# Shift rows of the first attention by one direct transfer, with one step less of lead

## The reference, cut to what matters

```python
qkv = x @ w_qkv.T                       # 16 heads, each with two sub-heads of width 4
def sdpa(qi, ki):
    s = jnp.einsum('bnhd,bmhd->bhnm', qi, ki) * scale
    p = jax.nn.softmax(s, axis=-1)
    return jnp.einsum('bhnm,bmhe->bhne', p, v)
o = sdpa(q[:, :, :, 0], k[:, :, :, 0]) - lam * sdpa(q[:, :, :, 1], k[:, :, :, 1])
```

## Time and profile before

| | |
|---|---|
| three runs | 1088.93, 1092.47, 1094.38 us (median 1092.47) |
| the profiled execution | 1090.65 us, its span 1088.8 us |
| busy over the span | PE 92%, DVE 88%, ACT 82%, POOL 45% |
| maxima on DVE | 512, 1208 ns each |
| exponentials on ACT | 1024, 600 ns each |
| first and last score matmul | 62.2 us, 652.6 us |

### The profile page before, as it was taken

How to read it: one execution, slowest core, us unless ns; L and a number is a source line. 1 busy time by engine, 2 the same in 40 slices (tenths; PEclk the granted TensorE clock), 3 DMA queues, 4 the chain that set the end, 5 groups by cost and what they waited for, 6 DMA issues and landing times.

```text
span 1088.8 us, 21671 instructions
## 1 busy us (share of the span) xinstructions
PE 1001.9 (92%) x8016; PEld 515.6 (47%) x8016; DVE 959.6 (88%) x1186; ACT 890.0 (82%) x1466; POOL 485.9 (45%) x893
## 2 busy tenths in 40 slices
PE   6389999999999999999999999999899999999998
PEld 3022222222222222222222236787677777777876
DVE  7799999999999999999999947798866988787665
ACT  5179999999999999999999987777775787678765
POOL 3363555455555544564556467342413431323331
PEclk9579999999999999999999999999999999999999
DMA  8911110111011101100110008575757466757763
GB/s 277 304 30 50 52 51 4 50 51 51 4 51 51 37 17 51 51 26 28 52 51 22 3 8 192 144 187 131 173 150 179 136 160 179 194 145 182 197 190 90
DMA packets 80473, 108.91 MB, mean 100 GB/s; under 512 B 23536, under 2 KB 33520, under 8 KB 80368
## 3 DMA queue, kind: packets, MB, share of 16 engines
q1 hardware_dynamic: 66336, 100.98, 34.4%
q10 hardware_dynamic: 14032, 6.55, 2.3%
HBM read 95.57 MB, written 11.93 MB: 99 GB/s over the span
## 4 chain that ended last, share of the span: by engine, by line
DVE 54%; PE 27%; ACT 7%; issue 6%; DMA 5%; POOL 1%; SPq 1%; ACTq 0%; DVEq 0%; POOLq 0%
DVE NEGMAX L1065 46%; PE PS L1456 7%; PE PS L1458 7%; PE PS L1457 7%; PE PS L1358 2%; DVE HF L1106 2%; DVE HL L1114 2%; ACT PR L858 2%; DMA GATE<-gate_d 1%; PE PS L1331 1%; ACT PS L955 1%; ACT HH L948 1%; ACT L955 1%; DVE ln_st L1000 1%; DMA shift_d<-SHT 1%
## 5 line engine op out<-in xcount | busy, mean ns | idle before, releaser
L1065 DVE TENSOR_REDUCE NEGMAX<-PS 128x1 f32<-128x1024 f32 x512 | 584.6, 1208 | 10.4 <-PE PS L1294 9.7
L858 ACT ACTIVATE PR<-PS 128x512 f32<-128x512 f32 x1024 | 538.9, 600 | 37.1 <-PE PS L1331 24.2
L1358 PE MATMUL PS<-PR,VG 128*32 128x256 f32 (+1 forms) x3840 | 321.3, 406 | 17.3 <-ACT PR L858 2.0
L1331 PE MATMUL PS<-QB,KB 32*128 32x512 bf16 x1024 | 260.1, 387 | 3.7 <-DMA QB<-shift_d 2.5
L1294 PE MATMUL PS<-KA,QA 32*128 32x512 bf16 x1024 | 204.3, 397 | 31.2 <-DVE NEGMAX L1065 22.4
L1106 DVE TENSOR_TENSOR HF<-PS,GATE 128x1024 f32<-128x1024 f32 x128 | 156.2, 1221 | 72.7 <-ACT PS L955 62.3
L1331 PEld LDWEIGHTS PS<-QB,KB 32*128 32x128 bf16 x1024 | 75.0, 91 | 239.8 <-ACT PR L858 137.4
L955 ACT ACTIVATE PS<-PS 128x1024 f32<-128x1024 f32 x128 | 129.2, 1010 | 71.5 <-PE PS L1458 70.9
L948 ACT ACTIVATE HH<-HF 128x1024 fp32r<-128x1024 f32 (+1 forms) x136 | 139.8, 1029 | 34.4 <-DVE HF L1106 32.6
L770 POOL TENSOR_TENSOR HL<-HF,HH 128x1024 fp32r<-128x1024 f32 (+1 forms) x32 | 69.2, 2162 | 165.8 <-ACT HH L948 165.8
L1358 PEld LDWEIGHTS PS<-PR,VG 128*32 128x32 f32 x3840 | 76.4, 108 | 130.7 <-issue 64.6
(11 more groups left out here) (186 smaller groups left out, 970.1 us busy)
## 6 DMA issues: line engine op xcount, KB each, us to landing
GATE<-gate_d SPq DMA_DIRECT2D x256, 256.0 KB, 4.1
QA<-q_stack SPq DMA_DIRECT2D x64, 128.0 KB, 2.6
QB<-q_stack SPq DMA_DIRECT2D x16, 256.0 KB, 2.9
KB<-k_stack SPq DMA_DIRECT2D x16, 256.0 KB, 3.0
KA<-k_stack SPq DMA_DIRECT2D x60, 64.0 KB, 2.4
q_stack<-PARTS SPq DMA_DIRECT2D x12, 256.0 KB, 4.4
k_stack<-PARTS SPq DMA_DIRECT2D x12, 256.0 KB, 4.6
RAWU<-in_L_ffn_W_up_dram ACTq DMA_DIRECT2D x4, 512.0 KB, 13.0
```

What stands on the lines that cost most here:

```text
L858: nc.scalar.activation(PR[:, s % PRING, r, :], PS[:, SCORE_BANK[n], :], ACT.Exp, scale=SCALE_A).then_inc(p_ready, 1)
L1065: nc.vector.tensor_reduce(NEGMAX[:, hs % 2, col:col + 1], PS[:, e:e + 2, :].rearrange("p b n -> p (b n)"), axis=AX_X, op=ALU.max, negate=T ...
L1331: mm(PS[:, SCORE_BANK[n], :], KB[strip, u, mt * P:(mt + 1) * P], QB[strip, u, half * BANK:(half + 1) * BANK], start=True, stop=True).then_ ...
L1358: last = mm(PS[STRIP * r:STRIP * (r + 1), 7, cols], VG[:, u, mt, r // 2, :], PR[:, s % PRING, r, cols], start=mt == 0, stop=mt == TB - 1 a ...
```

## The change

Four things change together. The stack layout becomes (4 rows d, 8 slots c) in place of (8 slots, 4 rows), with slots 6 and 7 constant, so that one DMA writes all slots of a part, and slot 7 of every strip receives the shift: rows 7, 15, 23, ... of `QB`. POOL lays the three parts out so (the fourth is zero), the transposition has 64 rows in place of 48, and one DMA goes from `SHT` to `QB` with nothing in DRAM between. LEAD is 11, and the side work of the last steps moves one step on. The transposition stands two steps ahead of the half in place of three, after the first value products in place of the end of the step, and DVE's copy stands at the start of that step, ahead of both maxima.

```diff
-LEAD = 12
+LEAD = 11
 def shift_at(g):
-    return (g + 3) // TB if (g + 3) % TB == 0 and 0 <= (g + 3) // TB < 2 * NG else None
+    return (g + 2) // TB if (g + 2) % TB == 0 and 0 <= (g + 2) // TB < 2 * NG else None
 SIDE = {
-    NQ - 12: [("heads_T", 0)], NQ - 11: [("proj", 0), ("stats", ("f", 0))], NQ - 10: [("norm", ("f", 0))],
+    NQ - 11: [("heads_T", 0)], NQ - 10: [("proj", 0), ("stats", ("f", 0))], NQ - 9: [("norm", ("f", 0))],
...
             def write_parts(b, part):
...
-                    for c in places:
-                        rows = stack[b * GPB:(b + 1) * GPB, :, HD_A * c:HD_A * (c + 1), :].rearrange("g r d n -> (g r) d n")
-                        sp.dma_start(rows, src).then_inc(st_w[b], 16)
+                    step = places[1] - places[0] if len(places) > 1 else 1
+                    rows = stack[b * GPB:(b + 1) * GPB].rearrange("g r d c n -> (g r d) c n")[:, places[0]:places[-1] + 1:step, :]
+                    sp.dma_start(rows, src.unsqueeze(1).to_broadcast([P, len(places), SEQ])).then_inc(st_w[b], 16)
...
             def shift_rows(s, half):
                 u, hs = s % 2, 2 * s + half
+                if half == 0:
+                    sp.wait_ge(sh_w, 16 * (s + 1))
                 sp.wait_ge(sht_ok, hs + 1)
-                sp.dma_start(shift_d[half].rearrange("a r (t n) -> (a r t) n", n=P), SHT[:, half, :]).then_inc(sh_w, 16)
-                sp.wait_ge(sh_w, 48 * s + 16 * (half + 2))
-                for r in range(R):
-                    lo = STRIP * r + SHIFT_ROW
-                    sp.dma_start(QB[lo:lo + 3, u, half * BANK:(half + 1) * BANK], shift_d[half, :, r, :]).then_inc(sh_r, 16)
+                sp.dma_start(QB[SHIFT_SLOT:P:SLOTS, u, half * BANK:(half + 1) * BANK], SHT[:, half, :]).then_inc(sh_r, 16)
...
             link(nc.gpsimd.memset(ZERO[:], 0.0))
+            link(nc.gpsimd.memset(SHP[:], 0.0))
             shift_parts(0)
...
             def max_quad(s):
+                if shift_at(s) is not None:
+                    shift_out(shift_at(s))
                 for key in quad_items(s):
...
-                    if key[2] == 0 and shift_at(s) is not None:
-                        shift_out(shift_at(s))
-                if not quad_items(s) and shift_at(s) is not None:
-                    shift_out(shift_at(s))
...
             def quad(s):
...
                 if valued:
                     weighted_values(s - 1, 0)
+                if shift_at(s) is not None:
+                    shift_tile(shift_at(s))
                 if scored:
                     scores(s, 2)
                 m_items(items[1:2])
                 if scored:
                     scores(s, 3)
-                if shift_at(s) is not None:
-                    shift_tile(shift_at(s))
```

More of the change, by code:

```diff
@@ L40 @@
 K_SLOTS = (2, 1, 0, 0, 0, 1)
-SHIFT_ROW = HD_A * len(Q_SLOTS)
 STRIP = 32
-STACK_WRITES = 16 * 2 * (len(Q_SLOTS) + 1)
+SLOTS = STRIP // HD_A
+SHIFT_SLOT = SLOTS - 1
+STACK_WRITES = 16 * 2 * 4
 MAX_LOADS = 16 * 2 * R
@@ L116, in score_tiles @@
                 tiles["out", output_at(g)] = len(tiles)
-        if shift_at(g) is not None:
-            tiles["shift", shift_at(g)] = len(tiles)
+            if p == 1 and shift_at(g) is not None:
+                tiles["shift", shift_at(g)] = len(tiles)
     return tiles
@@ L154 @@
 SIDE = {
-    NQ - 12: [("heads_T", 0)], NQ - 11: [("proj", 0), ("stats", ("f", 0))], NQ - 10: [("norm", ("f", 0))],
-    NQ - 8: [("x_T", ("f", 0))], NQ - 7: [("affinity", 0)], NQ - 6: [("top", 0)], NQ - 5: [("sum", 0)], NQ - 3: [("gate_T", 0)],
+    NQ - 11: [("heads_T", 0)], NQ - 10: [("proj", 0), ("stats", ("f", 0))], NQ - 9: [("norm", ("f", 0))],
+    NQ - 7: [("x_T", ("f", 0))], NQ - 6: [("affinity", 0)], NQ - 5: [("top", 0)], NQ - 4: [("sum", 0)], NQ - 2: [("gate_T", 0)],
     (0, 2): [("heads_T", 1)], (0, 4): [("proj", 1), ("stats", ("f", 1))], (0, 6): [("norm", ("f", 1))],
@@ L365, in hybrid_layer @@
         OTS = sb("OTS", [P, 2, BANK], where=attn)
-        SHP = sb("SHP", [P, 2, 3 * SHIFTS], BF16, where=attn)
-        SHT = sb("SHT", [3 * SHIFTS, 2, P], BF16, where=attn)
+        SHP = sb("SHP", [P, 2, R, 4, SHIFTS // R], BF16, where=attn)
+        SHT = sb("SHT", [4 * SHIFTS, 2, P], BF16, where=attn)
         ZERO = sb("ZERO", [P, SHIFTS], where=attn)
@@ L398, in hybrid_layer @@
         PS = ctx.enter_context(nc.psum_tensor("PS", [P, 8, BANK], F32))
-        q_stack = nc.dram_tensor("q_stack", (NG, R, STRIP, SEQ), BF16, kind="Internal").ap()
-        k_stack = nc.dram_tensor("k_stack", (NG, R, STRIP, SEQ), BF16, kind="Internal").ap()
+        q_stack = nc.dram_tensor("q_stack", (NG, R, HD_A, SLOTS, SEQ), BF16, kind="Internal").ap()
+        k_stack = nc.dram_tensor("k_stack", (NG, R, HD_A, SLOTS, SEQ), BF16, kind="Internal").ap()
         gate_d = nc.dram_tensor("gate_d", (2 * NCH, E, BANK), F32, kind="Internal").ap()
         mixed_d = nc.dram_tensor("mixed_d", (BATCH, S0, HD_B, HEADS_B, S1), F32, kind="Internal").ap()
-        shift_d = nc.dram_tensor("shift_d", (2, 3, R, BANK), BF16, kind="Internal").ap()
         ld_x = [sem(f"ld_x{c}") for c in range(NCH)]
@@ L470, in fill_shift_rows @@
                 for stack, fill in ((q_stack, ZEROS), (k_stack, ONES)):
-                    rows = stack[b * GPB:(b + 1) * GPB, :, SHIFT_ROW:STRIP, :].rearrange("g r s n -> (g r) (s n)")
-                    sp.dma_start(rows, fill[:].unsqueeze(1).to_broadcast([P, 2, SEQ])).then_inc(st_w[b], 16)
+                    rows = stack[b * GPB:(b + 1) * GPB].rearrange("g r d c n -> (g r d) c n")[:, len(Q_SLOTS):SLOTS, :]
+                    sp.dma_start(rows, fill[:].unsqueeze(1).to_broadcast([P, SLOTS - len(Q_SLOTS), SEQ])).then_inc(st_w[b], 16)
             def write_parts(b, part):
@@ L498, in load_strips @@
             def load_strips(stack, tile, u, g, there):
-                sp.dma_start(tile[:, u, :], stack[g].rearrange("r s n -> (r s) n")).then_inc(there, 16)
+                sp.dma_start(tile[:, u, :], stack[g].rearrange("r d c n -> (r d c) n")).then_inc(there, 16)
             def load_max(u, g, keys=True):
@@ L774, in _ @@
                 side(where)
-                if where == NQ - 11:
+                if where == NQ - 10:
                     heads_norm(2 * NG - 3)
@@ L1076, in shift_out @@
                 if hs >= 2:
-                    dve.wait_ge(sh_w, 48 * (hs // 2 - 1) + 16 * (hs % 2 + 2))
-                nc.vector.tensor_copy(SHT[:, hs % 2, :], PS[0:3 * SHIFTS, SCORE_BANK[n], 0:P // 2].bitcast(BF16)).then_inc(sht_ok, 1)
+                    dve.wait_ge(sh_r, 16 * (hs - 1))
+                nc.vector.tensor_copy(SHT[:, hs % 2, :], PS[0:4 * SHIFTS, SCORE_BANK[n], 0:P // 2].bitcast(BF16)).then_inc(sht_ok, 1)
             def evac_out(k):
@@ L1326, in scores @@
                 if q % TB == 0 and p == 0:
-                    pe.wait_ge(sh_r, 64 * (s // TB + 1))
+                    pe.wait_ge(sh_r, 16 * (s // TB + 1))
                 bank_free(n)
```

20 lines of the change are left out of this document (11 added, 9 removed).

## The result

| | before | after |
|---|---|---|
| median | 1091.01 us (6 runs, 1088.74 to 1094.38) | 1104.55 us (6 runs, 1103.39 to 1107.1) |
| ratio after / before | | 1.0126, 95% interval 1.0106 to 1.0145 |
| profiled execution | 1090.65 us | 1103.39 us |
| its span | 1088.8 us | 1101.5 us |

The change makes the kernel 1.3% slower. The two traces differ by 12.7 us of span. I cut both at the same events of the program; DVE's maxima and the first up projection are easy to find in each.

The account below looks back on a forecast made before the run. DVE was taken to pace the attention (busy 428.90 of 430 us). Wait +12.3, step -2.1, shifts -1.9, head 0 sum to +8.3 us: 1099.0 on the profiled execution, 1100.8 on the median; forecast 1100, range 1092 to 1108.

Parts of the forecast that it names:

- DVE waits 0.41 us for the transposition in 30 halves: Attention: DVE reaches its copy before PE's transposition, issued behind value products, is ready; 30 x 0.41 = +12.3 us.
- One step fewer, -2.1: End of attention: 11 steps instead of 12 remain after the last maximum, saving a plain step; -2.1 us, at least -1.8.
- The late shifts, -1.9: Attention: one direct DMA brings the shift in time, removing the excess of halves whose score 0 came late; -1.9 us.
- The two terms together: The 30 halves: DVE's wait for the transposition plus the gain on late shifts, +12.3 - 1.9 = +10.4 us.
- The head, 0 with 0.7 either way: Start: stack bytes unchanged, fewer issues save at most 0.5 us, an extra POOL memset costs about 0.3; net 0.
- the new wait on SP: SP waits until `QB` is loaded before sending the shift; costed at nothing, as that load is issued many steps earlier.
- a first copy late by a few tenths: Head: DVE reaches its first copy one maximum earlier while POOL's split ends later; nothing or a few tenths lost.
- The wait partly pays for itself: Rival, attention: 0.16 kept per half, so the wait is 0.25; +3.5 us in all, 1094 to 1096; chance 0.14.
- DVE does not wait: Rival, attention: ready maximum passes the copy or transposition comes in time; the 12.3 falls away, 1086.6 to 1088.5; chance 0.11.
- The direct transfer is late: Rival, attention: shift landings beyond 3.9 us cost each half the difference; 1109 at 4.2, 1137 at 5.1; chance 0.07.

Follow-up runs that it names:

- e1_early_tp: Changed kernel with PE issuing the transposition ahead of the step's first value products, copy still first on DVE; 1092.72 us, ratio 1.002.
- e2_late_tp: Changed kernel with the transposition at the end of its step, behind score 3, copy still first on DVE; 1118.05 us, ratio 1.025.
- e5_mid_copy: Changed kernel with 12 small stack writes per batch and DVE's copy behind the step's first maximum, transposition left in place; 1092.55 us, ratio 1.0008.
- e4: Changed kernel with the transposition ahead of the value products and 12 small stack writes per batch; 1091.14 us, ratio 1.0005.
- e9: e4 with two of the four loads of the up weights issued at the start of ACT's program; 1099.81 us, ratio 1.0075.
- e6_lead12: Changed kernel with LEAD 12, transposition and copy at their old places, direct transfer kept, 12 small stack writes per batch; 1091.57 us, ratio 1.0006.
- e7: Changed kernel with LEAD 12, transposition and copy at their old places, direct transfer and 6 joined stack writes per batch kept; 1094.95 us, ratio 1.0027.
- e3: Changed kernel with 12 stack writes of 256 KB per batch in place of 6 larger ones, new layout kept; 1104.57 us, ratio 1.0132.
- e8: Same kernel as e3, run again: changed kernel with 12 small stack writes per batch; 1102.98 us, ratio 1.0109.
- e12: e4 with one of the four loads of the up weights issued at the start of ACT's program; 1092.91 us, ratio 1.0017.
- e11: Changed kernel with early transposition, joined stack writes and two of the four up-weight loads at the start of ACT's program; 1097.9 us, ratio 1.0071.
- e10: e4 with all four loads of the up weights issued at the start of ACT's program; 1101.85 us, ratio 1.0107.

## Why the prediction was right, and where it was not

**DVE waits 0.41 us for the transposition in 30 halves: right.** The wait is 0.41 in half 12, from the two durations that the prediction used (0.57 from the products to the transposition, 0.28 from it to the copy). The steady half grew by 0.42 (18.74 - 18.32), and 30 x 0.42 = 12.6. e1_early_tp took it away, e2_late_tp doubled it, e5_mid_copy took it away at the other end.

**One step fewer, -2.1: right,** measured -2.20. The gates are 0.63 and 1.02 late for DVE, which the rest of the program absorbs. The runs with 12 steps show 28.0 us from the last maximum to the first up projection, those with 11 show 25.8 (e4 and e9 27.3, for another reason, below).

**The late shifts, -1.9: right.** The two terms together were +10.4 and measured +11.11. In e6_lead12, without the wait, the 30 halves gain 1.71 (551.49 - 549.78). I had taken 2.9 us for the landing, and misread the row: it tells of the 16 loads of 256 KB from `q_stack` into `QB`, while the 128 small reads from `shift_d` have no landing in that view, so nothing in it was near in kind, the 5.1 of the last rival neither. The landing is 1.8, and nothing hung on the difference. The Trainium skill ("DMA: Bandwidth & Descriptors", section on the anatomy of one DMA) gives about 2.0 us as the fixed cost on another issuing path; the 1.8 measured here on SP's queue lies near it.

**The head, 0 with 0.7 either way: this step failed,** by 3.7 us (-0.65 + 4.36). It was argued from bytes: they don't change, the DMA engines are full, so fewer issues save at most the ramp. That is true of the stacks, and the first maximum did start 0.65 us earlier. What it leaves out is who shares the engines. The loads on ACT's queue lie beside the stack writes; with joined writes they landed in 18.5 to 19.4 us in the median (after, e1, e2, e7), with small ones in 12.9 to 15.2 (e3 to e6 and e8), before in 13.0, and the last of them, which counts, 0.4 to 4.2 us later with joined writes than with small ones. The conversion stands ahead of the first exponential and is ACT's to do, so their lateness goes into the attention. I had looked at ACT's row of exponentials in mid-attention and not at what ACT does before its first one.

A term that was put at nothing failed there too, the new wait on SP. In mid-attention it costs nothing: but for half 0, SP issues each shift within 0.1 us of the copy's end. In the head `QB`'s load landed 7.4 us after its issue, the shift went out 1.4 us behind the copy, and score 0 waited 1.27 us for it.

How the lateness of the conversion turns into loss can be read down the table. In after, e1, e2, e3, e5, e7 and e8 ACT goes from its conversions straight to its first exponential. There the head's loss is the delay of the conversion behind the first maximum less 19.4 us, in all seven within 0.9 (e3 19.48, e8 19.49, after 19.49, e7 19.79; the extremes are e1 with 18.64 and e2 with 20.30): a conversion one us later costs about one us. In before, e4 and e6 ACT was idle for the scores (1.88, 0.63 and 0.90 us), as it was in e9 to e12, so their loss of 0.88 to 2.67 has other causes. Two stand in their traces. All seven wait 0.9 to 1.6 us behind the first value products at the lower clock: 0.9 where it rises about 3 us behind the first of them (before, e9), 1.2 to 1.6 where it takes 3.4 to 5.9 us. What decides when it rises was not found; it does so at 72.0 in e6, where ACT is not late, and at 68.7 in e3, where it is. And e4 and e12 wait 0.90 and 0.68 at the copy of half 0.

The lead has a part in this. Only kernels with 11 steps wait at the copy of half 0 (e4, e5, e8 and e12, 0.39 to 1.08 us, all with small writes; e2 by its own edit), and only they have score 0 wait for its shift (after, e1 to e5 and e8, 0.8 to 2.2 us of PE), which costs DVE 0.33 us after the change and 1.25 in e1. The three with 12 steps (before, e6, e7) have neither. The prediction had allowed for a first copy late by a few tenths; in the changed kernel's own trace it is on time.

How large the gain of small writes is on the time stays open. By medians it is 0.0 and 1.6 (after against e3 and e8), 1.6 (e1 against e4) and 3.4 (e7 against e6), with two loads issued early it is -1.9 (e11 against e9), and the intervals overlap in each pair. Why the conversion starts 1.7 us later in e8 than in e3, the same kernel, was not found. Nor was the old layout of the stacks run with the new order, so the layout's own part in the head isn't separated.

**The rivals.** *The wait partly pays for itself* is refuted: the halves lose all of it, once and doubled. *DVE does not wait* is refuted by the thirty waits; the condition that it was tied to, a transposition issued 0.41 earlier, is what e1_early_tp makes true, and there the halves are at 18.32. But e1 has 1092.72 and not the 1086.6 to 1088.5 that I gave this case; the head is most of the difference. *The direct transfer is late* did not occur, with 2.6 at most against a limit of 3.9.

**Did the change have something to give?** The step saved at the end and the late shifts are worth 4.0 us by the prediction, 2.2 + 1.7 by the traces. With the wait and the large writes mended (e4_early_split) the median is that of before, 1.0005 (0.9991 to 1.0018). Against before, its trace has the first maximum 0.69 us earlier, half 0 to 1 1.42 longer, the 30 halves 1.32 shorter, the end 0.73 shorter (the clock's dip, below, takes 1.5 of the 2.2), and the feed-forward part 1.88 longer, where the change touches nothing. So of what the change gives, the head takes a part back, and what stays is no larger than what one execution differs from the next. No version here is measurably faster than the kernel before.

## What to carry to other kernels

When a small job is moved on the engine that sets the pace, work out when that engine comes to it and when its input is there, with all that now stands ahead of the producer on its own engine: an in-order engine that is never idle loses each late tenth in full in every round, and one ready instruction ahead of the consumer, or one matmul behind the producer, mends it. "The same bytes" doesn't mean the same time when two queues share the DMA engines: ask which other load lies in that window, and what stands behind the engine that needs it. A term that is nothing in the steady state must be looked at once more in the first round, where loads land late and PE's clock may be low. And a load issued earlier has a price on the engine that issues it, so look at the time of the issue before moving it ahead of first work.

## What the runs showed of the hardware that was not expected

A DMA of 16 KB from SBUF to SBUF landed in 1.8 us from its issue (min 1.8, max 2.6 over the 32 of the changed kernel), and its issue is listed with 0.58 us on SP.

Issuing 512 KB loads held the issuing engine: 13.72 us for two of them on ACT (e9), 18.59 us for four (e10), while in the trace nothing else is named as what ACT waits for. The first row shows e10's issue, the second what ACT did next:
```profile
7.49 18.59 ACTq L802 DMA_DIRECT2D RAWU<-in_L_ffn_W_up_dram  x4
26.13 1.08 ACT L793 ACTIVATE XT<-PS 128x512 f32<-128x512 f32 x2 [19.03 <-issue]
```

PE's granted clock fell for a few microseconds near the end of the attention in some executions. The table of busy time by stretch has it at 0.53 in e4_early_split:
```profile
635.00:638.00 3.00, 2.94 (x14) 0.94 (x14) 1.80 (x3) 1.32 (x3) 2.56 (x6) 0.53 0.00 0
```
The 0.53 of that stretch is close to the lower of its two levels, 1.2 of 2.4 GHz. The same group of eight value products took 1.94 us there and 1.06 us in e3_split, where the clock was full:
```profile
636.00 1.94 PE L1356 MATMUL PS<-PR,VG 128*32 128x512 f32 x8
```
```profile
648.86 1.06 PE L1356 MATMUL PS<-PR,VG 128*32 128x512 f32 x8
```
In the 3 us ahead of these stretches PE was busy for 2.42 us in e4_early_split and for 2.45 in e3_split, at the full clock in both, so these rows don't tell the two executions apart. The end of the attention is 1.5 us longer in the two traces that have this dip (e4 and e9, 27.3) than in the other nine with 11 steps (25.8). The feed-forward part, where no edit changes anything, takes 434.0 to 440.9 us over the fourteen traces. The dips in it don't explain that by themselves: e3_split and e8_split_again, the same kernel, have one short dip each there, ahead of the program's end, and take 435.0 and 439.1. What else differs was not found. This spread is as large as the effects of the head, and is why the medians of 12 runs say less about the head than the traces do.
